# Sends and first projections of a half moved, in a four-layer attention and expert kernel on one core

## The reference

```
x = x + tanh(g_xattn[0]) * cross_attention(layernorm(x), ctx)        # att0, 16 heads of 8, 512 keys
x = x + tanh(g_ffn[0])   * moe_top1(layernorm(x))                     # moe0: 8 experts, 128 -> 512 -> 128
x = x + tanh(g_xattn[1]) * decoder_block(layernorm(x), ctx)           # att1 (256 keys), att2 (512 keys), ffn
x = x + tanh(g_ffn[1])   * rope_block(x)                              # att3 (causal), moe1: 4 experts, top 2
```

## Time and profile before

| | |
|---|---|
| median of 3 runs | 1208.27 us (1203.97 to 1213.19) |
| the profiled execution, its own time | 1199.09 us, span 1197.3 us |
| PE busy | 1058.3 us (88% of the span) |
| DVE busy | 791.6 us (66%) |
| ACT busy | 620.4 us (52%) |
| POOL busy | 370.3 us (31%) |
| granted clock of PE, mean | 0.941 of full speed |

### The profile page before, as it was taken

One profiled execution on the slowest core, in us unless ns is written; L12 is line 12 of the kernel. 1 busy time (PEld: TensorE's weight loads), 2 busy tenths in 40 slices (PEclk: granted clock), 3 DMA queues, 4 the chain that ended last, 5 costly groups with the idle time before them and its releaser, 6 DMA issues. The chain is left out here.

```text
span 1197.3 us, 25289 instructions
## 1 busy us (share of the span) xinstructions
PE 1058.3 (88%) x8548; PEld 651.4 (54%) x8548; DVE 791.6 (66%) x1935; ACT 620.4 (52%) x1331; POOL 370.3 (31%) x982
## 2 busy tenths in 40 slices
PE   4999998799998797788899998987988889899998
PEld 1455554477554585444455544444555667656665
DVE  4688887534867424677688869688574776645443
ACT  1477665455664454565477755655544445543221
POOL 4333332221434323434333324322242434200000
PEclk9999998899986898898899998999979899999999
DMA  6655644453434572656655544433334456201000
GB/s 160 192 159 175 176 148 137 153 174 112 130 109 135 161 227 61 192 155 190 193 169 172 158 134 141 136 109 115 106 118 131 125 158 181 75 22 45 10 27 10
DMA packets 173174, 157.98 MB, mean 132 GB/s; under 512 B 13075, under 2 KB 146835, under 8 KB 172691
## 3 DMA queue, kind: packets, MB, share of 16 engines
q1 hardware_dynamic: 168854, 141.24, 39.8%
q0 software_dynamic: 4192, 15.12, 4.0%
HBM read 91.56 MB, written 66.85 MB: 132 GB/s over the span
## 5 line engine op out<-in xcount | busy, mean ns | idle before, releaser
L1102 ACT ACTIVATE prob<-ps 128x512 f32<-128x512 f32 (+1 forms) x768 | 398.9, 578 | 171.5 <-PE ps L1664 128.6
L1296 DVE TENSOR_REDUCE nmax<-ps 128x1 f32<-128x512 f32 x512 | 328.5, 684 | 88.8 <-PE ps L1629 86.8
L1664 PE MATMUL ps<-Qst,Kst 75*128 75x256 bf16 x1408 | 244.4, 285 | 8.6 <-DMA Qst<-mrow 5.8
L1680 PE MATMUL av_ps<-prob,Vx 128*32 128x256 f32 (+1 forms) x3072 | 218.3, 401 | 0.0
L1629 PE MATMUL ps<-Kst,Qst 72*128 72x512 bf16 x512 | 198.2, 403 | 21.7 <-DVE nmax L1296 19.5
L1664 PEld LDWEIGHTS ps<-Qst,Kst 75*128 75x128 bf16 x1408 | 137.0, 102 | 76.4 <-ACT prob L1102 11.8
L1680 PEld LDWEIGHTS av_ps<-prob,Vx 128*32 128x32 f32 x3072 | 92.8, 115 | 67.7 <-issue 38.7
L1026 POOL TENSOR_TENSOR mparts<-nmax,zeros 128x8 bf16<-128x8 f32 x122 | 24.8, 203 | 311.8 <-issue 305.1
L1305 DVE TENSOR_REDUCE nmax<-ps 128x2 f32<-128x512 f32 x128 | 85.9, 687 | 48.5 <-PE ps L1643 47.7
L1106 ACT ACTIVATE OT<-av_ps 128x256 f32<-128x256 f32 x128 | 49.2, 385 | 116.4 <-PE av_ps L1680 116.1
L1629 PEld LDWEIGHTS ps<-Kst,Qst 72*128 72x128 bf16 x512 | 50.5, 99 | 102.2 <-DVE nmax L1296 47.6
(11 more groups left out here) (198 smaller groups left out, 1667.0 us busy)
## 6 DMA issues: line engine op xcount, KB each, us to landing
q_parts<-qp SPq DMA_DIRECT2D x96, 192.0 KB, 2.6
Qst<-q_parts SPq DMA_DIRECT2D x128, 144.0 KB
k_parts<-kp SPq DMA_DIRECT2D x46, 384.0 KB, 3.4
Kst<-k_parts SPq DMA_DIRECT2D x60, 288.0 KB
k_parts<-kp SPq DMA_DIRECT2D x48, 192.0 KB, 2.7
Kst<-k_parts SPq DMA_DIRECT2D x64, 144.0 KB
ctxT<-in_ctxT SPq DMA_DIRECT2D x16, 256.0 KB, 4.8
xs_rows<-in_blank SPq DMA_DIRECT2D x22, 128.0 KB, 4.0
```

Source lines behind the costliest of these rows:

```text
L1102: act.activation(prob[:, RING_AT[st] % RING, half * 512:half * 512 + w], bank(x)[:, 0:w], ACT.Exp).then_inc(drained(x), 1)
L1296: ve.tensor_reduce(nmax[:, g, u, h % GH:h % GH + 1], bank(st), AX.X, ALU.max, negate=True).then_inc(drained(st), 1)
L1664: last = pe.matmul(o, Ks[0:KROWS, par, h, t * P:t * P + P], Qst[0:KROWS, par, h, :], start=True, stop=not a.rope)
L1680: last = pe.matmul(av_ps[VW * hh:VW * hh + VW, SQ - w:SQ], Vx[:, par, t, h, :], prob[:, place, off * SQ:off * SQ + w], start=(t == 0), sto ...
```

## The change

The plan of a half moves to position 13, behind its last ranks; its first weight read and its eight sends start at 14 instead of 16, the three other weight reads stand at 18 instead of 20. The tiles of half 0 begin at 26 instead of 24 (those of half 1 stay), and with them all that follows the tiles of half 0, by two positions. For batches 8 and 12, K is projected ahead of Q, both at one position; Q is split on DVE at its store step instead of on POOL; the statistics of batch 9 and 13 come one position behind them, and both stores stand at one position. `sends_beside` changes which maxima are split on DVE: before (5,2), (5,3), (9,2), (9,3), (13,2), (13,3); after it (5,1), (5,2), (5,3), (7,0), (9,1), (9,2), (9,3), (11,0), as batch and group of four heads. In bodies 4 and 8 V of the next batch stands at 12 instead of 10, and the load of x and its statistics three positions earlier.

```diff
         for k in range(3):
-            put(n, 14 + k, ("m0.plan", g, k))
-        put(n, 16, ("m0.wload", g, 0))
+            put(n, 13, ("m0.plan", g, k))
+        put(n, 14, ("m0.wload", g, 0))
         for j in range(GT):
-            put(n, 16 + j // 2, ("m0.scatter", g, j))
+            put(n, 14 + j // 2, ("m0.scatter", g, j))
         for k in range(1, WRING):
-            put(n, 20, ("m0.wload", g, k))
+            put(n, 18, ("m0.wload", g, k))
...
-        put(n, p + 6, ("q", m, None), ("qsplit", m, None), ("xstat", m + 1, None))
-        put(n, p + 7, ("k", m, None), ("ksplit", m, 0))
-        put(n, p + 8, ("qstore", m, None))
-        put(n, p + 9, ("kstore", m, None))
+        put(n, p + 6, ("k", m, None), ("ksplit", m, 0), ("q", m, None), ("qsplit", m, None))
+        put(n, p + 7, ("xstat", m + 1, None))
+        put(n, p + 8, ("qstore", m, None), ("kstore", m, None))
...
+def plans(n):
+
+    return 0 < n <= B and n % HALF == 0
...
 def sends_beside(n, arg):
-    return n <= 2 * B - HALF + 1 and n % HALF == 1 and n > HALF and arg >= 2
+    return HALF < n < 2 * B - HALF and (n % HALF == 1 and arg >= 1 or n % HALF == HALF - 1 and arg == 0)
...
-TILES_AT = (24, 26)
+TILES_AT = (26, 26)
...
-        put(12 if a.rope else 10, ("v", n + 1, None))
+        put(12 if a.rope or plans(n) else 10, ("v", n + 1, None))
...
-            put(8, ("loadx", n + 3, None))
-            put(14, ("xstat", n + 3, None))
+            put(5 if plans(n) else 8, ("loadx", n + 3, None))
+            put(11 if plans(n) else 14, ("xstat", n + 3, None))
...
# POOL
-                if kind == "qsplit" and n and not sends_near(n):
+                if kind == "qsplit" and n and not (sends_near(n) or opens_half(n)):
# DVE
-                elif kind == "qstore" and sends_near(n):
+                elif kind == "qstore" and (sends_near(n) or opens_half(n)):
# PE
-                    if ("xT", n, None) in BANK and kind == "q":
+                    if ("xT", n, None) in BANK and kind == ("k" if opens_half(n) else "q"):
```

## The result

The changed kernel takes 1222.53 us at the median of five runs (1220.41 to 1229.74) against 1208.27 for the kernel before: ratio 1.0126, 95% interval 1.0085 to 1.0168. I had said 1205.5, in 1192 to 1216. It is slower by 10 to 14 us at the medians, 12 to 16 by the ratios. (Medians are over all executions of a kernel; ratios leave out those over 1.5% slower than its fastest, two of them near 3319 us, and need not be the ratio of the medians.)

The account below looks back on a forecast made before the run. It took PE, 88% busy, and its waits, four of them 17.9 us together, to bound the kernel; the terms summed to -2.8 us, from a median of 1208.3 to 1205.5 us, range 1192 to 1216.

Parts of the forecast that it names:

- Head of half 0, -5.0 and -1.2: First tile of half 0: PE's 5.03 us wait for the sent rows goes, -5.0; the low clock around it, -1.2.
- Head of half 1, -2.0: First tile of half 1: sends 2 us sooner take -2.0 off PE's 4.63 us wait for the rows.
- The maxima and Q split on DVE, +1.0, +1.5, +1.0: Added DVE work: maxima (5,1) +1.0; Q split of batch 8 with (7,0) +1.5; maxima (9,1) +1.0.
- the sign that I gave for being wrong: Bodies 6 and 7: new waits of PE on DVE of over 3 us together would show the prediction wrong.
- xstat one position later: Body 11: xstat(13), moved behind the last scores' maxima, helps put Q's split at 482.6; no size of its own.
- Batches 8 and 9: Where DVE is full: Q split of batch 8 costs 1.7 us and (7,0) 1.0, partly covered, so +1.5.
- (11,0) on DVE, 0: Body 10's 3.97 us wait: (11,0) is done in time, but PE then waits for DVE behind it, so 0.
- K and Q of batch 12, +3.4: Body 11: SP stores Q first, after a late DVE split, so the wait for K ends 3.4 us later.
- the bound of 6: Upper bound of the term for K and Q of batch 12 in body 11: +6 us.
- Batch 13, -1.5: Maxima (13,2) and (13,3) leave a busy DVE for an idle POOL: -1.5 us.
- The rule that I weighed: DVE two-input and GpSimd SBUF instructions exclude each other; a Q split could wait twice, sum 1.4 us higher; left out.
- the one that ended slower, at 1213.7: Rival: weight reads' bytes decide when the first tile lands; both heads keep waits, DVE work adds, +5.4 us; chance 0.15.

Follow-up runs that it names:

- c1: The kernel before, unaltered, measured in the third set of runs: 1209.99 us, one run.
- a3: The kernel before with only the tiles of half 0 moved to 26 from 24: 1211.62 us, ratio 0.9998.
- b4: The kernel before with only plan, sends, weight reads, V and statistics of batch 7 and 11 moved as in the change: 1199.87 us, ratio 1.0000.
- d3: The changed kernel with plan, sends, weight reads, V and loads where they were before: 1214.66 us, ratio 1.0207 to before.
- d4: The changed kernel with the maxima split where they were before: 1212.75 us, ratio 1.0161 to before.
- b1: The kernel before, unaltered, measured in the second set of runs: 1197.73 us, ratio 1.0022.
- b2: The kernel before with tiles of half 0 at 26 and sends and weight reads one in a position: 1199.31 us, ratio 1.0026.
- d1: The kernel before with tiles at 26 and sends and weight reads one in a position, measured in the fourth set: 1195.32 us, ratio 1.0027.
- c2: The changed kernel, unaltered, measured in the third set of runs: 1221.45 us, ratio 1.0101 to before.
- c4: The changed kernel without its part of Q and K, in the third set: 1213.31 us, ratio 1.0028 to before.
- e2: The changed kernel, unaltered, measured in the fifth set of runs: 1226.28 us, ratio 1.0110 to before.
- a2: The kernel before with the change's part of Q and K alone: 1220.09 us, ratio 1.0070.

## Why the prediction was wrong, step by step

- **Head of half 0, -5.0 and -1.2: the step that failed first.** The wait for the rows goes in all profiles of the change, as I said, and the first send follows the last rank by 4.0 us (200.04 to 204.05) where it took 7.5; in this profile it comes no sooner than before, as the rank is itself 3.4 us later. But 2.78 us of waiting for V stand in its place, a term that my sum didn't have: I moved the first tile to the position where V is projected and looked at its rows alone. And the gain was taken from the one profile shown. The runs of before beside the change, 1208.27 at the median, are near the sets with stops (1211.5 to 1212.5) and not the others (1196), so most of them will have had the stop in place of the wait (they have no profile; this is inferred). `c1` has no wait to remove, and `a3` changes nothing: 0.9998. Without the stop before waits 5.03, 4.14 and 1.8 us there in its three profiles, and `b4`, `d3` and `d4`, which wait less for the rows, don't beat it either.
- **Head of half 1, -2.0.** Wrong where it can be seen: with the sends earlier 5.39 (`b4`) and 5.65 us (`d4`) are left in place of 4.4 to 4.8. In `b4` the last send ends at 389.64, SP issues the load at 394.95 and it takes 8.2 us, in `b1` 7.2: its issue hardly follows the sends. That the load is slow behind the weight reads I had right: the DMA share is 0.98 from 216.7 to 225.8 in the profile of the earlier trace rows, and in `b2` and `d1`, with the weight reads spread out, the same loads take 2.0 to 2.3 us.
- **The maxima and Q split on DVE, +1.0, +1.5, +1.0.** The new waits of PE on DVE are of the size I gave, 1.8 us in body 7; I priced them at their length. With the clock behind them body 7 alone is +2 to +8. Bodies 6 and 7 together have the sign that I gave for being wrong, new waits of PE on DVE of over 3 us: 2.84, 1.53 and 1.83 us in `c2` where `c1` has one of 1.14; the first two come with tiles at 26 (`c4`: 2.87 and 1.44). No term of my sum had a clock for a *new* wait, though the earlier trace rows show it behind an old one and I counted it there as a gain.
- **xstat one position later.** I followed it for batch 13 and not for batch 9, where it meets the tiles' two positions. Batches 8 and 9 should have been worked out on the queues of body 7, as batch 12 was on those of body 11.
- **(11,0) on DVE, 0.** Right: the transpose doesn't wait, the score behind it waits 2.2 us for row maxima (3.2 and 3.3 in `c2` and `e2`).
- **K and Q of batch 12, +3.4.** Right in mechanism and order, SP and DVE as foretold, K's store 3.8 us later in the body (I had 3.4); the body is some 5 us longer (4.3 to 5.5 against `c1`, 6.0 between the first two profiles), about the bound of 6. Wrong in how it shows: not as a longer wait for K but as xn, rows and a low clock ahead of it.
- **Batch 13, -1.5.** Not isolated; it is below what the bodies behind it vary by.
- The rule that I weighed (the Trainium skill, SBUF — State Buffer, section Who interferes with whom) would have added 1.4 us by my estimate. In `e2` the split of Q in body 7 begins when POOL has ended, and its subtractions take 0.43 us as in the earlier trace rows. DVE's two-input addition of 328.08, which ran into POOL's split of K, took 0.69 us where the same one took 0.48. In `a2` the same addition began with 0.53 us of POOL's subtraction left, in place of 0.41, and took 0.81 us. So the two do hold each other up, by 0.2 to 0.3 us here, and the rule decided nothing.

Of the rivals, the one that ended slower, at 1213.7, had the direction and less than half the size (heads keep their cost, DVE's work is added), by another mechanism. The sum with the heads' gains struck is -2.8 + 5.0 + 1.2 + 2.0 = +5.4; body 7 at 8.2 where batches 8 and 9 had +1.5, and body 11 at 5 where it had +3.4, would add 8.3 more. That is fitted to two profiles afterwards and shows nothing by itself.

**Left open.** What the stop is: it stands in all profiles of three sets, on three chips, and in none of two sets, on one of the same chips, whatever the kernel; the paced sends ran only without it. Two explanations don't fit `c1`: from 209 to 213, as it begins, the DMA share is only 0.15, and no packet of the queues that load instructions starts between 197 and 222 us. Why the clock falls behind the wait of body 7 in some executions and not in others is open too. How the whole change stands to before without the stop wasn't measured; `d3` and `d4`, at +2.1 and +1.6%, suggest no better. No version tried beats before. The obvious next one, the change with the statistics of batch 9 and 13 back ahead of K and Q, wasn't run.

## What to carry to other kernels

Price a new wait of PE by what can follow it: here 1.8 us of waiting cost 8 us where 12 us at the lower clock came behind it, in `c2`, `e2` and `d4`, and 2 us where none did, in `d3` and the first profile. A change that trades long waits for several short ones can remove all that it aims at and lose. When a step moves, look at every engine that it then meets, not only at the one it was late for: the first tile got its rows and met V. And before counting a wait as gain, see it in more than one execution: the profile shown was 9 us quicker than the median, and three profiles of the same kernel without the stop have 5.0, 4.1 and 1.8 us there.

## What the hardware did that I hadn't expected

While POOL issued twelve indirect transfers, the last eleven 1.28 us apart, PE, DVE and ACT could stand still together, for 7 to 8 us in one piece (`c1`, 211 to 219) or in several shorter ones, in both halves. In each of the twenty-two stops (eleven profiles, two halves) the last of these waits of ACT and DVE ends 2.0 to 2.4 us behind POOL's last transfer. In other sets of runs nothing of the kind happened with the same instructions at the same times. The medians of before are 1211.5 to 1212.5 us in the sets with it and 1196.0 to 1196.2 without.
